# A gated cross-attention kernel: the subtract and scale of the second norm as one ScalarE activation for each token tile

## The reference

```python
def _layernorm(x, axis=-1, eps=1e-05):
    m = jnp.mean(x, axis=axis, keepdims=True)
    v = jnp.var(x, axis=axis, keepdims=True)
    return (x - m) / jnp.sqrt(v + eps)

x = x + jnp.tanh(g_xattn[0]) * _L0_xattn_ref(_layernorm(x, axis=-1), ctx_768, ...)
x = x + jnp.tanh(g_ffn[0]) * _L0_ffn_ref(_layernorm(x, axis=-1), ...)
```

## Time and profile before

| what | us |
|---|---|
| median of 3 runs | 1948.74 |
| lowest, highest | 1944.63, 1948.91 |
| the profiled execution, its own time | 1939.76 |
| its span | 1938.0 |
| TensorE matmul busy | 1878.5 (97%) |
| VectorE busy | 1323.6 (68%) |
| ScalarE busy | 1241.6 (64%) |
| GpSimd busy | 146.8 (8%) |

### The profile page before, as it was taken

How to read it: one execution, slowest core, us unless ns; L and a number is a source line. 1 busy time by engine, 2 the same in 40 slices (tenths; PEclk the granted TensorE clock), 3 DMA queues, 4 the chain that set the end, 5 groups by cost and what they waited for, 6 DMA issues and landing times.

```text
span 1938.0 us, 25839 instructions
## 1 busy us (share of the span) xinstructions
PE 1878.5 (97%) x8916; PEld 1350.1 (70%) x8916; DVE 1323.6 (68%) x2341; ACT 1241.6 (64%) x2083; POOL 146.8 (8%) x320
## 2 busy tenths in 40 slices
PE   7999999999989999999999999999999999999998
PEld 6733433333458777888888788888878888887886
DVE  6798888888747787556665655666565566556555
ACT  4457777677753334667676776676676666767665
POOL 6201001101113430000000000000000000000000
PEclk9979999999989999999999999999999999999999
DMA  8933232222111164222433322342332333322331
GB/s 285 363 81 84 76 89 70 81 78 74 58 54 77 77 250 146 97 109 90 157 118 115 109 88 109 120 154 93 112 109 87 121 144 122 112 89 87 109 109 56
DMA packets 97245, 220.84 MB, mean 114 GB/s; under 512 B 31314, under 2 KB 49492, under 8 KB 87892
## 3 DMA queue, kind: packets, MB, share of 16 engines
q1 hardware_dynamic: 97108, 219.12, 32.6%
HBM read 178.57 MB, written 40.24 MB: 113 GB/s over the span
## 4 chain that ended last, share of the span: by engine, by line
PE 68%; DVE 2%; issue 1%; ACT 1%; POOL 0%; DVEq 0%; ACTq 0%
PE ps_y L2137 32%; PE ps_h L2084 28%; PE ps_h L2057 4%; PE ps_y L2069 4%; DVE h_hi L2431 0%; DVE out_T_acc L2527 0%; DVE candidate_c L2489 0%; DVE h_lo L2435 0%; ACT gelu L2329 0%; DVE gated L2520 0%; DVE more_early L2539 0%; DVE early L2583 0%; DVE gate L2479 0%; ACT w_first_hi L2229 0%; ACT w_pair L2282 0%
## 5 line engine op out<-in xcount | busy, mean ns | idle before, releaser
L2435 DVE TENSOR_TENSOR h_lo<-gelu,h_hi 128x512 fp32r<-128x512 f32 x512 | 354.5, 697 | 407.0 <-ACT h_hi L2332 405.9
L2084 PE MATMUL ps_h<-x_hi,w_pair 128*128 128x512 f32 x1568 | 562.4, 392 | 1.6 <-ACT gelu L2329 0.8
L2329 ACT ACTIVATE gelu<-early,b 128x512 f32<-128x512 f32 x336 | 243.2, 724 | 229.2 <-DVE early L2583 220.2
L2084 PEld LDWEIGHTS ps_h<-x_hi,w_pair 128*128 128x128 f32 x1568 | 294.2, 188 | 77.5 <-issue 5.6
L972 DVE TENSOR_REDUCE low<-ps_s 128x1 f32<-128x512 f32 x512 | 321.5, 683 | 30.3 <-PE ps_s L813 27.9
L2332 ACT ACTIVATE h_hi<-gelu 128x512 fp32r<-128x512 f32 x448 | 283.5, 633 | 42.5 <-ACT gelu L2329 1.5
L2084 PE MATMUL ps_h<-x_lo,w_pair 128*128 128x512 f32 x784 | 309.2, 394 | 0.0
L1142 ACT ACTIVATE probs_T<-ps_t 128x512 f32<-128x512 f32 x384 | 207.8, 600 | 98.9 <-PE ps_t L824 97.3
L2583 DVE TENSOR_TENSOR early<-ps_h,copy 128x512 f32<-128x512 f32 x336 | 230.6, 686 | 48.2 <-PE ps_h L2084 48.1
L813 PE MATMUL ps_s<-k_st,q_st 48*128 48x512 f32 x512 | 204.1, 475 | 3.4 <-SPq L724 2.0
L2137 PE MATMUL ps_y<-h_hi,w_lo 128*128 128x512 f32 x512 | 202.6, 396 | 0.0
(11 more groups left out here) (262 smaller groups left out, 2598.1 us busy)
## 6 DMA issues: line engine op xcount, KB each, us to landing
x_hi<-blocks_scratch SPq DMA_DIRECT2D x28, 1024.0 KB, 5.1
x_lo<-blocks_scratch SPq DMA_DIRECT2D x28, 1024.0 KB, 8.8
x_hi<-blocks_scratch SPq DMA_DIRECT2D x28, 768.0 KB, 6.7
x_lo<-blocks_scratch SPq DMA_DIRECT2D x28, 768.0 KB, 10.2
gate<-gates_scratch SPq DMA_DIRECT2D x64, 256.0 KB, 3.2
q_st<-q_scratch SPq DMA_DIRECT2D x192, 64.0 KB, 2.3
k_st<-k_scratch SPq DMA_DIRECT2D x192, 64.0 KB, 2.3
k_scratch<-k_hl SPq DMA_DIRECT2D x8, 1024.0 KB, 5.4
```

Source lines behind the costliest of these rows:

```text
L2084: mm = pe.matmul(bank, w[wp], x[xp], start=start and n == 0, stop=n == 2, skip_group_check=not start)
L2329: act.activation(gelu[:, c % GELUS, :], src, ACT.Gelu_apprx_tanh, bias=b1[p][:, j:j + 1]).then_inc(gelu_done, 1)
L2435: dve.tensor_tensor(h_lo[:, j % RING, :], gelu[:, j % GELUS, :], h_hi[:, j % RING, :].bitcast(F32), ALU.subtract).then_inc(h_ready, 1)
```

## The change

In `attend_programs`, for batches 0 to 6, the instruction that writes `xn` moves from VectorE (`tensor_scalar`, subtract then multiply) to ScalarE (`activation` Identity with a column as scale and a column as bias). The bias column is minus mean times the reciprocal root: GpSimd negates the mean where it made it, and adds one product, `shift`, at the end of its chain. There is one more row in `moments`, and one more count of `moment_done` for each batch. On ScalarE the two activations of step (2, 0), and the two of (2, 1), stand behind the first two exponentials of the step and behind the unit taken there. The last batch's norm stays on VectorE.

```diff
-    moments = n_.sb("moments_b", [P, 10, TT])
+    moments = n_.sb("moments_b", [P, 11, TT])
...
-            first = b * 9
+            first = b * 10
...
-            pool.tensor_scalar(mean, root, 0.5, 0.0, ALU.mult, ALU.add).then_inc(moment_done, 1)
+            pool.tensor_scalar(mean, root, -0.5, 0.0, ALU.mult, ALU.add).then_inc(moment_done, 1)
...
-            pool.tensor_tensor(rstd, root, dev, ALU.add).then_inc(rstd_done, 1)
+            pool.tensor_tensor(rstd, root, dev, ALU.add).then_inc(moment_done, 1)
+            pool.wait_ge(moment_done, first + 10)
+            pool.tensor_tensor(shift, mean, rstd, ALU.mult).then_inc(rstd_done, 1)
...
                     kind, i = NORM_STEPS.get((g, k), (None, 0))
-                    if kind and exists(b - 1):
-                        {"statistics": statistics, "normalised": layer_norm}[kind](b - 1, i)
+                    if kind == "statistics" and exists(b - 1):
+                        statistics(b - 1, i)
...
+        def layer_norm(b, i):
+            if i == 0:
+                act.wait_ge(rstd_done, b + 1)
+                wait(act, in_psum["xnT"], b * KT)
+            for t in (2 * i, 2 * i + 1):
+                ins = act.activation(xn[:, t, :], x_res[:, t, :], ACT.Identity, bias=moments[:, 10, t:t + 1], scale=moments[:, 9, t:t + 1])
+            ins.then_inc(xn_ready, 1)
...
                     if (g, k) != (0, 0):
                         take_unit(b, STEPS[STEPS.index((g, k)) - 1] + (1,))
+                    kind, i = NORM_STEPS.get((g, k), (None, 0))
+                    if kind == "normalised" and exists(b - 1):
+                        layer_norm(b - 1, i)
                     back = group_after(b, g, -1)
                     if k == 0 and exists(back[0]):
                         copy_out(*back)
```

More of the change, by code:

```diff
@@ L759, in reciprocal_root @@
         def reciprocal_root(b):
-            mean, dev, diff, square, spread, var, root, root_2, scaled, rstd = (moments[:, i, :] for i in range(10))
-            first = b * 9
+            mean, dev, diff, square, spread, var, root, root_2, scaled, rstd, shift = (moments[:, i, :] for i in range(11))
+            first = b * 10
             pool.wait_ge(stats_done, b * 2 + 2)
@@ L800, in gpsimd @@
         last = [moments[:, i, :] for i in range(10)]
-        pool.wait_ge(moment_done, LAST * 9 + 3)
+        pool.wait_ge(moment_done, LAST * 10 + 3)
         pool.tensor_tensor(last[6], last[5], exponent[:], ALU.pow).then_inc(moment_done, 1)
@@ L1019, in last_variance @@
             mean, dev, diff, square, spread, var, root, root_2, scaled, rstd = (moments[:, i, :] for i in range(10))
-            first = LAST * 9
+            first = LAST * 10
             dve.wait_ge(stats_done, BATCH * 2)
```

## The result

The changed kernel takes 1969.88 us (median of 4 runs, 1966.27 to 1970.27), the kernel before beside it 1946.78 us. The ratio on record, which is not exactly the quotient of the two medians, is 1.0115, with a 95% interval from 1.0095 to 1.0134. By the medians it is 23 us slower, where 4.8 were forecast and 1960.0 was the upper end of the range. The direction was right; the size and the range were wrong.

The account below looks back on a forecast made before the run. Prediction: ScalarE, then VectorE 5 us later, limit TensorE in steps (2, 0) and (2, 1). Six batches at 0.62 us plus 1.09 for batch 7 make 4.8 us, giving 1953.5 us, range 1945.5 to 1960.

Parts of the forecast that it names:

- D: Time two activations hold ScalarE, forecast 0.98 us; as a rival's letter: semaphore wait breaks ScalarE's back-to-back issue, 2 us, 1955.5.
- the shift and the table loads: GpSimd's extra product, 0.28 us later, is hidden by 0.5 us; ScalarE has no more table loads, so nothing added.
- the walk: Timeline of batch 3 through steps (2, 0) and (2, 1) with the activations added: first `xnT` 0.62 us late each batch.
- VectorE's relief: The norm taken off VectorE, 1.3 us a batch, said to absorb 0.24 to 0.28 us of TensorE's 0.86 to 0.90.
- Batch 7: Last host batch, without scores of a further batch: VectorE gives nothing back, `ps_o` starts 1.09 us late.
- low D: Two activations hold ScalarE only 0.54 us: about 0.1 us a batch and 1 us in all.
- rival C: No difference: ScalarE's 0.70 us gap and VectorE's relief take the activations; 0 to 1 us, 1949 us; chance 0.15.
- A: Rival: VectorE's queue is what counts, so the kernel gets faster by at most 9 us, 1939.6 us; chance 0.07.
- B: Rival: nothing is absorbed, ScalarE's extra 13.7 us land in full on TensorE, 1962.4 us; chance 0.11.

Follow-up runs that it names:

- e9: Changed kernel with only the first pair of activations, step (2, 0), on ScalarE and the second pair on VectorE; ratio to the kernel before 1.0134.
- e10: Changed kernel with only the second pair of activations, step (2, 1), on ScalarE and the first pair on VectorE; ratio to the kernel before 1.0004.
- e3: Changed kernel with GpSimd's shift kept but the norm of every batch on VectorE; ratio to the kernel before 0.9997.
- e11: Changed kernel plus four unread reductions of 128x256 a batch on VectorE at the old norm's place; one run, 1960.74 us.
- e0: The changed kernel run again without alteration; ratio to the kernel before 1.0116.
- e5: Changed kernel with the activations as plain copies, without scale and bias columns, subtraction and scaling left out; ratio to the kernel before 1.0055.
- e6: Changed kernel plus 31 unread TensorE products in groups 2 and 3 of batch 7; ratio to the kernel before 1.0065.

## Why the prediction was wrong, and where it was right

**Right: what bounds these steps.** Both helpers at their limit within 5 us, ScalarE first. e9 and e10 show it.

**Right: the price.** D was put at 0.98 us and measured 0.98; 587 ns were forecast and 596 measured.

**Right: the shift and the table loads cost nothing** (e3; as many loads as before, and no wait for GpSimd).

**Right: the walk for batches 1 to 6.** 0.62 us a batch forecast, 0.61 measured, with TensorE's wait at the place named. The minima that the walk put at 307.08 and 307.69 start at 307.07 and 307.68 (4.38 taken off). VectorE's two gaps are there, but both at step (2, 1), none at (2, 2). One sentence in it was wrong: that VectorE's relief absorbs 0.24 to 0.28 us. e11 gives the relief back and the period stays. What absorbed it was slack that VectorE has as soon as TensorE is late; the old norm would have fitted in there too.

**Wrong: batch 7.** The step that failed is "*Batch 7*", with its 1.09 us. ScalarE's part of it is right: in e0 the exponentials in question end at 540.10, 20.55 us behind the first copy of the batch, and the walk has 20.56. TensorE's 1.09 itself can't be read off, since the clock falls before it in every trace with that wait. What the step had wrong is that it took TensorE's clock as given. The first part of the prediction had read it as full in batches 2 and 3 and never asked whether a longer wait would change it, although the trace of before has it at 0.91 from 540 to 550 us and at 0.75 from 550 to 560, at the end of this very batch. The fall, 38 us at the lower clock in the profiled execution and about 25 in the second, cost 14.34 - 1.09 = 13 us in the one and 8.59 - 1.09 = 7.5 in the other: more than all that was forecast. It is also the larger part of why the sum for a low D was wrong (the other is the 0.28 us a batch): e5, near the point where rival C should have won, measured 1.0055.

**Missed as well: short spells.** All six traces in which both columns are used and the first pair is on ScalarE in batches 1 to 6 had batches with a mean clock of 0.94 to 0.97, one to four of them, at 1.4 to 2.8 us each (e6: 59.03 us for 56.21); 18 in all. In all 18 the clock falls 17.3 to 18.3 us behind the batch's first copy, that is 0.2 to 1.2 us behind the end of TensorE's wait of 1.15 us for ScalarE, which ends at 17.1. In e0, batch 2, the wait ends at 248.23:

```profile
243.40:248.40 5.00, 3.85 (x27) 1.59 (x25) 4.61 (x9) 4.78 (x10) 1.77 (x8) 1.00 0.34 109
248.44:251.84 3.40, 3.40 (x15) 0.71 (x13) 1.02 (x2) 2.64 (x7) 0.00 (x0) 0.50 0.45 112
```

Of the ten other traces three had one such batch each, with the fall some 41 us behind the first copy, and none fell at the place of the wait. So the short spells and the long fall of batch 7 start at the same wait. In batches 1 to 6, where scores of a later group stand beside the products, the clock is back after 3.4 or 6.8 us. The same wait is there in the other 18 of these 36 batches too, without a fall; what decides between them is open.

**The rivals.** A was out in sign: no faster kernel came of VectorE's relief at this place, though e10, with two of the four instructions taken off VectorE, has batches 0.28 us shorter. That VectorE's relief is what shortens them is argued, not shown by a run. B, at 1962.4, lay nearest to the time, and for the wrong reason: ScalarE's 13.7 us did not land in full (0.61 of 1.96 a batch did). C was out by the price of 596 ns; e5, near its condition, had 0.28 us a batch and the fall. D did not happen: the activations start 0.48 us behind `out_T_acc`, as closely as the others, and its 0.3 us a batch had no row.

**The range.** It ended below the price of B and had no room for a mechanism that no term named.

## What to carry to other kernels

Read where an instruction lands, not how busy the engine is: the same 0.98 us cost 0.6 us a batch ahead of a chain without a gap, and a batch was 0.28 shorter with it one step later, next to engines that were equally busy. Before a change that makes TensorE wait longer, look for places where it works alone and thinly and where its granted clock already dips: a wait of 1.2 us there was followed by 25 to 38 us at half clock, which cost six to eleven times the wait, and one of 0.8 us (e5) could do the same. An edit of a repeated loop should be checked in its last iteration by itself, since the work that ran beside is missing there.

## What the runs showed of the hardware

- The granted clock fell behind a wait of 1.16 us, in a stretch in which no scores of a later group run beside TensorE's products, and stayed down for the rest of attention (in e0 it fell at the same wait, was down for 20.5 us, came back for 6.8 and fell again). Before the fall TensorE was busy in the records for 3.76 of 5 us (first row). In batch 3 it was busy just as much around the same wait (second row), and the clock stayed full. In the kernel before, at the like place of batch 7, it was 4.72 (third row):

```profile
530.00:535.00 5.00, 3.76 (x21) 1.31 (x23) 1.02 (x4) 4.78 (x11) 1.31 (x7) 1.00 0.00 0
303.76:308.76 5.00, 3.77 (x28) 1.32 (x29) 4.22 (x10) 4.78 (x11) 1.33 (x7) 1.00 0.33 89
521.77:526.77 5.00, 4.72 (x27) 1.41 (x24) 2.32 (x8) 4.61 (x11) 1.10 (x6) 1.00 0.00 0
```

  At the lower clock TensorE's busy share then rises (36.91 of 38.29 us), so the share does not show the loss. The Trainium skill, page "TensorE: Matmul & The Clock Gate", section "Part 1: The HAM clock gate (the "warmup" mystery)", has the clock follow how busy TensorE has been of late; by that rule, which the prediction left out, a kernel that keeps it busier keeps more of the clock. e6 agrees in part: its clock still fell behind the wait, for 3.4 us.
- Matmuls that nobody reads can shorten a stretch: batch 7 of the changed kernel took 44.23 us with 237 matmuls and 50.3 to 56.1 with 206. In the kernel before the same products gained nothing that could be measured (0.9995).
- A scale and a bias column cost an activation of 128x256 182 ns together (596 against 414), and back to back two of them hold ScalarE for 0.98 us.
